# A two-layer graph network on one core: both layers in one program body, the first E tiles made ready earlier, and softmax row sums from fp16 halves

## The reference

```python
h = relu(layernorm(x))
x = x + A @ (h @ W0 + b0) / deg[:, None]          # A = (adj != 0), deg = column sums of A
h = relu(layernorm(x))
ht = (h @ W1) per head                            # 4 heads of 512
e = leaky_relu(src[:, None] + dst[None, :], 0.01) + adj
att = softmax(e, axis=-1)
x = x + mean over heads of att @ ht
```

## Time and profile before

| what | value |
|---|---|
| median of 3 runs | 2573.07 us |
| the profiled execution, its own time | 2572.89 us |
| its span, first to last instruction | 2571.2 us |
| TensorE busy | 2484.8 us, 97% |
| VectorE busy | 1878.0 us, 73% |
| ScalarE busy | 1244.6 us, 48% |
| GpSimd busy | 82.5 us, 3% |
| granted TensorE clock, mean | 0.979 |

### The profile page before, as it was taken

One profiled execution on the slowest core, in us unless ns is written; L12 is line 12 of the kernel. 1 busy time (PEld: TensorE's weight loads), 2 busy tenths in 40 slices (PEclk: granted clock), 3 DMA queues, 4 the chain that ended last, 5 costly groups with the idle time before them and its releaser, 6 DMA issues.

```text
span 2571.2 us, 42822 instructions
## 1 busy us (share of the span) xinstructions
PE 2484.8 (97%) x12301; PEld 1234.5 (48%) x12301; DVE 1878.0 (73%) x2621; ACT 1244.6 (48%) x1850; POOL 82.5 (3%) x132
## 2 busy tenths in 40 slices
PE   6989999599999999999999999999999999999997
PEld 3434446444444444444444444444444444444786
DVE  7779756497677876778677776777766877667774
ACT  4534544464444544445445454454444554444563
POOL 0000000000000000000000000000000000000000
PEclk9999998599999999999999999999999999999999
DMA  4175655400022000220002100021000300001000
GB/s 143 52 247 183 226 157 181 152 4 4 0 66 64 27 4 0 81 71 4 4 8 82 62 4 4 17 84 51 4 4 24 94 33 2 2 17 43 26 1 9
DMA packets 74145, 144.18 MB, mean 56 GB/s; under 512 B 4414, under 2 KB 11840, under 8 KB 72895
## 3 DMA queue, kind: packets, MB, share of 16 engines
q1 hardware_dynamic: 74047, 143.08, 17.4%
HBM read 129.37 MB, written 13.70 MB: 56 GB/s over the span
## 4 chain that ended last, share of the span: by engine, by line
PE 79%; issue 0%; DVE 0%; ACT 0%; POOLq 0%; POOL 0%
PE z_ps L1266 68%; PE o_ps L1290 11%; PE c_ps L1281 1%; DVE t_reg L1172 0%; ACT e_reg L1059 0%; DVE e_reg L1160 0%; DVE hl_reg L1138 0%; DVE ao_reg L1212 0%; DVE z_reg L1188 0%; ACT z_reg L1095 0%; POOLq L1029 0%; POOL ticks L1030 0%; POOLq L1030 0%; POOLq L352 0%
## 5 line engine op out<-in xcount | busy, mean ns | idle before, releaser
L1266 PE MATMUL z_ps<-hl_reg,h_reg 128*128 (+2 forms) x8736 | 1758.4, 364 | 23.9 <-DVE hl_reg L1138 23.9
L1266 PEld LDWEIGHTS z_ps<-hl_reg,h_reg 128*128 (+1 forms) x8736 | 855.3, 98 | 923.5 <-DVE hl_reg L1138 24.2
L1083 ACT ACTIVATE hl_reg<-t_reg (+2 forms) x364 | 361.7, 994 | 744.2 <-DVE t_reg L1172 399.8
L1138 DVE TENSOR_TENSOR hl_reg<-t_reg,hl_reg (+2 forms) x364 | 417.5, 1147 | 229.3 <-ACT hl_reg L1083 227.2
L1068 ACT ACTIVATE t_reg<-ring_reg,vv 128x512 f32 (+3 forms) x728 | 526.4, 770 | 71.0 <-DVE ao_reg L1153 59.0
L1172 DVE SCALAR_TENSOR_TENSOR t_reg<-t_reg,vv,e_reg (+3 forms) x728 | 510.4, 742 | 14.0 <-issue 8.2
L1153 DVE TENSOR_TENSOR ao_reg<-ao_reg,t_reg 128x1024 f32<-128x1024 f32 (+1 forms) x336 | 383.7, 1142 | 0.0
L1290 PE MATMUL o_ps<-w_reg,z_reg 128*128 128x512 f16 x1248 | 273.9, 379 | 0.6 <-DVE z_reg L1188 0.6
L1290 PEld LDWEIGHTS o_ps<-w_reg,z_reg 128*128 128x128 f16 x1248 | 121.9, 99 | 141.7 <-DVE z_reg L1188 0.7
L1188 DVE SCALAR_TENSOR_TENSOR z_reg<-z_ps,z_reg 128x512 f16<-128x512 f32 (+1 forms) x112 | 73.2, 653 | 147.6 <-ACT z_reg L1095 147.6
L1059 ACT ACTIVATE e_reg<-e_reg (+2 forms) x91 | 90.7, 996 | 176.1 <-DVE e_reg L1160 176.1
(11 more groups left out here) (126 smaller groups left out, 1072.0 us busy)
## 6 DMA issues: line engine op xcount, KB each, us to landing
ring_reg<-adjT_in SPq DMA_DIRECT2D x78, 512.0 KB, 4.2
e_reg<-adjT_in SPq DMA_DIRECT2D x78, 512.0 KB, 3.7
ring_reg<-x_in SPq DMA_DIRECT2D x13, 512.0 KB, 4.1
x_dram<-ring_reg SPq DMA_DIRECT2D x13, 512.0 KB, 6.4
ring_reg<-c_dram SPq DMA_DIRECT2D x24, 256.0 KB, 3.2
ao_reg<-x_dram SPq DMA_DIRECT2D x6, 1024.0 KB, 5.6
out_dram<-ao_reg SPq DMA_DIRECT2D x6, 1024.0 KB
w_reg<-W_in SPq DMA_DIRECT2D x5, 1024.0 KB, 9.7
```

Of the source, the lines that this page charges most:

```text
L1083: nc.scalar.activation(hl_ring[:, g % HL_RING, 0, :, 0:W], t_ring[:, g % T_RING, :, 0:W], ACT.Copy).then_inc(hi_ready, 1)
L1138: nc.vector.tensor_tensor(hl_ring[:, g % HL_RING, 1, :, 0:W], t_ring[:, g % T_RING, :, 0:W], hl_ring[:, g % HL_RING, 0, :, 0:W], ALU.subtr ...
L1266: mm = nc.tensor.matmul(z_ps[:, k, 0:W], hk[hs], hl_ring[:, r, ps, u, 0:W], start=first and u == 0 and n == 0, stop=last and u == 1 and n ...
```

## The change

1. The second block is gone. Its five engine programs become functions (`layer2_sync`, `layer2_gpsimd`, `layer2_scalar`, `layer2_vector`, `layer2_tensor`) that are called at the end of each engine's program in the first block, so that no engine waits there for all others. The memsets that give the semaphores their first credits stand at the start of VectorE's program. SyncE waits for the last stores of x1 before it reads `c` back, not after.
2. GpSimd's ticks are semaphore increments instead of adds. One add, `warm`, stands behind the last `partition_all_reduce`.
3. For block 0, VectorE subtracts the maximum from the E tiles of pairs 0 to 3 before the scores are taken out of PSUM, and of pairs 4 to 6 behind the tail's last VectorE instruction. It waits for the DMAs itself there. ScalarE takes the exponentials of pairs 0 to 3 before those of the tail (L804), and 4 to 6 after the copy (L808). Inside the first segment the rest follow two pairs ahead.
4. The row sums: `p_acc` is scaled by 2^-5 and split into fp16 halves at the end of a segment, by one ScalarE and one VectorE instruction (128x512) placed behind those that take out the last bank. TensorE does 8 fp16 matmuls in place of 4 fp32 ones, and does them behind the first 12 matmuls of the product instead of ahead of them.

```diff
-COEF = 1.0 / (ZS * HS * WS * H)
+RS = 2.0 ** -5
+COEF = RS / (ZS * HS * WS * H)
...
+acc16 = p_acc[:, :, 1].bitcast(F16).rearrange("p a (s i) -> p a s i", s=2)
...
+        E_PRE = LOOP0 + 2
+        E_PRE0 = 4
...
             if h == 0 and isinstance(b, int) and b == 0:
-                return (b, p + 1) if looped or p < PAIRS - 1 else None
+                return (b, p + E_PRE - LOOP0) if looped else None
...
             def pairs_here(b, p0, p1):
                 for p in range(p0, p1):
                     pool.wait_ge(e_in[p], (b + 1) * 16)
                     pool.wait_ge(mb_in, (b + 1) * 16)
-                    nc.gpsimd.tensor_tensor(ticks[:, p:p + 1], ones32[:], ones32[:], ALU.add).then_inc(e_here, 1)
+                    pool.sem_inc(e_here, 1)
...
         def subtract_max(dve, b, p):
+            if isinstance(b, int) and b == 0 and isinstance(p, int):
+                dve.wait_ge(e_in[p], 16)
+                dve.wait_ge(mb_in, 16)
+            else:
                 dve.wait_ge(e_here, b * PAIRS + p + 1)
...
             def evacuate(b, h):                     # ScalarE
...
+                act.wait_ge(acc_sum, q + 1)
+                nc.scalar.activation(acc16[:, h % 2, 0, 0:W], p_acc[:, h % 2, 0, 0:W], ACT.Copy,
+                                     scale=RS).then_inc(acc_hi, 1)
...
             def evacuate_z(b, h):                   # VectorE
...
+                dve.wait_ge(acc_hi, q + 1)
+                nc.vector.scalar_tensor_tensor(out=acc16[:, h % 2, 1, 0:W], in0=p_acc[:, h % 2, 0, 0:W],
+                                               scalar=RS, in1=acc16[:, h % 2, 0, 0:W], op0=ALU.mult,
+                                               op1=ALU.subtract).then_inc(acc_lo, 1)
...
-                pe.wait_ge(acc_sum, q + 1)
-                pe.wait_ge(rs_sb, q + 1)
-                for it in range(n):
-                    mm = nc.tensor.matmul(c_ps[:, it:it + 1], p_acc[:, h % 2, 0, it * P:(it + 1) * P],
-                                          ones32[:], start=True, stop=True)
-                mm.then_inc(rs_ps, 1)
+            def row_sums(b, h):
+                pe.wait_ge(acc_lo, q + 1)
+                pe.wait_ge(rs_sb, q + 1)
+                for it in range(width(b) // P):
+                    for s in range(2):
+                        mm = nc.tensor.matmul(c_ps[:, it:it + 1], acc16[:, h % 2, s, it * P:(it + 1) * P],
+                                              ones16[:], start=s == 0, stop=s == 1)
+                mm.then_inc(rs_ps, 1)
...
                     mm.then_inc(o_done, 1)
+                    if it == 0:
+                        row_sums(b, h)
...
                 nc.gpsimd.partition_all_reduce(dall[:], dmx[:], P, RMAX).then_inc(s_dall, 1)
+                nc.gpsimd.tensor_tensor(warm[:], ones32[:], ones32[:], ALU.add)
+                layer2_gpsimd(pool)
...
                 for j in pairs_of(NG1 - 1):
                     split1(j)
+                for p in range(E_PRE0):
+                    subtract_max(dve, 0, p)
                 dve.wait_ge(sd_ps, NT)
...
                 max_rows(1, IT)
+                for p in range(E_PRE0):
+                    exp_e(act, 0, p)
                 act.wait_ge(s_dn, 1)
```

More of the change, by code:

```diff
@@ L133, in gnn_kernel @@
         credits = sb("credits", 16, F32)
-        ticks = sb("ticks", PAIRS, F32)
+        warm = sb("warm", 1, F32)
         bst = sb("bst", NT * 6, F32)
@@ new lines, in o_before, with e_of @@
+        def o_before(b, h):
+            if isinstance(b, int) and b == FULL:
+                return FULL * H * IT + h * (LASTW // P)
+            return (b * H + h) * IT
+        def e_of(b, h, p):
+            looped = not isinstance(p, int)
+            if h == 0 and isinstance(b, int) and b == 0:
+                return (b, p + E_PRE - LOOP0) if looped else None
+            if h == 0:
+                return (b, p + E_LATE) if looped or p == LOOP0 - 1 else None
+            if h == H - 1 and (not isinstance(b, int) or b < FULL):
+                return (b + 1, p - LOOP0) if looped else None
+            return None
@@ new lines, in blocks, with exp_e, subtract_max @@
+        def blocks(eng, body, first=0):
+            for b in range(first):
+                body(b)
+            with eng.Fori(first, FULL - 1) as b:
+                body(b)
+            body(FULL - 1)
+            body(FULL)
+        def exp_e(act, b, p):
+            W = width(b)
+            act.wait_ge(e_sub, b * NT + p * 2 + 2)
+            e = e_blk[:, bass.ds(p * 2, 2), 0:W]
+            nc.scalar.activation(e, e, ACT.Exp).then_inc(e_ready, 1)
+        def subtract_max(dve, b, p):
+            W = width(b)
+            if isinstance(b, int) and b == 0 and isinstance(p, int):
+                dve.wait_ge(e_in[p], 16)
+                dve.wait_ge(mb_in, 16)
+            else:
+                dve.wait_ge(e_here, b * PAIRS + p + 1)
+            for u in range(2):
+                e = e_blk[:, p * 2 + u, 0:W]
+                nc.vector.tensor_tensor(e, e, max_bc[:, 0:W], ALU.subtract).then_inc(e_sub, 1)
@@ new lines, in layer2_gpsimd, with pairs_here, add_halves, body @@
+        def layer2_gpsimd(pool):
+            def pairs_here(b, p0, p1):
+                for p in range(p0, p1):
+                    pool.wait_ge(e_in[p], (b + 1) * 16)
+                    pool.wait_ge(mb_in, (b + 1) * 16)
+                    pool.sem_inc(e_here, 1)
+            def add_halves(b, h):
+                W = width(b)
+                pool.wait_ge(acc_done, (b * H + h + 1) * PAIRS + T_RING)
+                nc.gpsimd.tensor_tensor(p_acc[:, h % 2, 0, 0:W], p_acc[:, h % 2, 0, 0:W], p_acc[:, h % 2, 1, 0:W],
+                                        ALU.add).then_inc(acc_sum, 1)
+            pairs_here(0, 0, PAIRS)
+            def body(b):
+                for h in range(H - 1):
+                    add_halves(b, h)
+                more = not isinstance(b, int) or b < FULL
+                if more:
+                    pairs_here(b + 1, 0, LOOP1 - LOOP0)
+                add_halves(b, H - 1)
+                if more:
+                    pairs_here(b + 1, LOOP1 - LOOP0, PAIRS)
+            blocks(pool, body)
@@ L436, in _ @@
                 sp.dma_start(c_dram.rearrange("h (t i) -> (h t) i", i=P), c_st[0:H * NT]).then_inc(cr_out, 16)
+                for i in range(PAIRS - ADJ_RING, PAIRS):
+                    sp.wait_ge(x1_out[(NA + i) % ADJ_RING], 16 * (i // ADJ_RING + 1))
                 sp.wait_ge(cr_out, 16)
@@ L439, in _ @@
                     load_c(sp, 0, h)
[L440 to L441 removed]
                 sp.wait_ge(mr_out, 48)
                 load_x1(sp, 0)
+                layer2_sync(sp)
             @block.gpsimd
@@ L687, in _ @@
                 link(dve, nc.vector.tensor_scalar(vv4[:, 2], vv4[:, 0], -1.0, None, ALU.mult))
+                for p in range(E_PRE0, E_PRE):
+                    subtract_max(dve, 0, p)
+                layer2_vector(dve)
             @block.scalar
@@ L808, in _ @@
                 nc.scalar.activation(c_st[0:H * NT], o_ps[0:H * NT, 0, 0:P], ACT.Copy).then_inc(cr_sb, 1)
+                for p in range(E_PRE0, E_PRE):
+                    exp_e(act, 0, p)
+                layer2_scalar(act)
             @block.tensor
```

595 lines of the change are left out of this document (272 added, 323 removed).

## The result

The changed kernel takes **2547.09 us** (median of 4 runs, 2546.13 to 2548.46) against 2572.86 for the kernel before on the same chip (4 runs): ratio 0.9901, 95% interval 0.9884 to 0.9918. That is 25.8 us less.

What follows compares the result with a forecast made beforehand. TensorE, busy 97% of the span, was taken to bound the kernel, so only its wait before the segments and the row sums could pay: 2572.9 - 10.0 - 9.1 = 2553.8 us, range 2548 to 2562.

Steps and rivals of the forecast that it cites:

- The bound: Whole kernel: TensorE, busy 97% of the span, sets the time; its one long wait, 23.9 us, precedes the segments.
- The seam: From the tail to the segments' first matmul: TensorE starts at 501.1 in place of 511.14, 10.0 us less.
- My bound for neither `vv` nor `c` moving: Tail to segments: with both unmoved, TensorE would start at 497.6, 13.5 us less.
- The row sums: In each segment: 8 fp16 passes take 0.42 us in place of 0.79; 9.1 us less over all.
- 53 ns a pass: fp16 row sums: the clock-scaled part of a 98 ns weight load sets each pass's pace; the other 45 ns overlap.
- The rival: Row sums nearly free, a pass at half of 53 ns or less: 0.2 us a segment, 2549 us, chance 0.12.
- Layer 0: Work before the segments: the forecast sum has no term for a change in its length.
- What I costed at nothing: Segments: one more ScalarE and VectorE instruction each, 0.6 and 0.69 us, hidden under 5.7 us of cover, 2.9 in narrow ones.
- The range: Whole time: 2548 to 2562 us, from nearly free row sums up close to row sums that give nothing.
- The bound itself (a pass that costs nothing, -20): Row sums: if a pass cost nothing, they would give 20 us less.

Runs made afterwards that it cites:

- e2: The kernel before with one edit, GpSimd's ticks as semaphore increments instead of adds: 2564.05 us (6 runs), 0.9965 of before.
- e3: The changed kernel with the two blocks back, so that all engines meet between the tail and the segments: 2547.49 us.
- e10: The changed kernel with ScalarE's exponentials of E for pairs 0 to 3 moved behind the copy, pairs 4 to 6 into the first segment: 2544.93 us (4 runs).
- e15: The kernel of e10 run again, side by side with e14: 2544.16 us (4 runs).
- e6: The changed kernel with 24 more fp16 one-column passes in each segment, weights of 128 columns, results never read: 2564.91 us.
- e7: The changed kernel with 24 more fp16 one-column passes in each segment, weights of 127 columns: 2588.24 us.
- e12: The changed kernel with 24 more fp16 one-column passes in each segment, weights of 96 columns: 2577.32 us.
- e9: The changed kernel with 24 more fp16 passes of 128 moving columns in each segment: 2584.78 us.
- e8: The changed kernel with 24 more fp32 one-column passes (12 matmuls) in each segment, weights of 128 columns: 2661.46 us.
- e14: The changed kernel itself run again, side by side with e15: 2547.84 us (4 runs).
- e4: The changed kernel without GpSimd's add `warm`: 2547.15 us.

## Why the prediction was wrong, step by step

- **The bound**, TensorE alone in the segments and one long wait at the seam: right. The 10.38 and 67.34 us of a period are the same before and after.
- **The seam**, 10.0 us forecast, 10.27 measured. The chain is the forecast one: `vv` from 485.62 to 488.15 with the last split 1.24 us earlier, so 3.8 us later (forecast 3.9); `rows_c` 3.3 us later (forecast 3.5); `c` 3.2 us after it is asked for; 5.2 us from `c` to TensorE (forecast 5.2). e2 shows that the ticks alone carry 9.6 of it, e3 that the meeting carries 0.15, e10 that the exponentials ahead of `c` cost 3.0 of what else would be gained. My bound for neither `vv` nor `c` moving, 13.5 us less, is nearly what e10 reaches (13.3) and e15 (12.9).
- **The row sums**, "53 ns a pass": the step that failed. Forecast 9.1 us less, measured 15.25 over all segments. With 0.18 us a segment the sum gives 24 x 0.61 + 3 x 0.26 - 0.1 = 15.3. The term was mis-sized: the row sums take 0.18 us a segment, 22.5 ns a pass, where I had 0.42. I had taken the part of a load's recorded length that changes with the clock, 53 of 98 ns, for the pace of a stream of loads, and only the other 45 for what overlaps. e6, e7 and e12 show what sets the price: a pass with the full 128 fp16 columns costs 24 ns, and with fewer the price goes column by column, about one cycle of 2.4 GHz each, 43 ns for 96 and 57 for 127. The 53 ns are near the price of the slower load, for one that takes the faster. Whether that faster load sets the 24 ns or something else that no pass here went below was not separated. The recorded length is 72 to 85 ns above the price in every kind of one-column pass that was run; I had let 45 ns of it overlap.
- **The rival.** I had the right number beside me. The Trainium skill (TensorE: Matmul & The Clock Gate, Back-to-back issue gap) gives about 25 ns for a matmul of 1 to 64 columns, and its section Weight-path perf modes says that a fast load is used for 128 weights of a type other than fp32. Both agree with the traces: 24 ns, and 57 with 127 columns. The first section's 81 ns for a stream with 128 moving columns does not agree with e9, 56 ns. I gave the rival of nearly free row sums a chance of 0.12 because the 53 seemed to come from this case's rows, and it is what came. I had also summed it wrongly. At 0.2 us a segment, 24 x 0.59 + 3 x 0.24 - 0.2 is 14.7 us less, so that the whole is 2548.2, and not the 2549.6 that stands beside the 25 ns, nor quite the 2549 of the rival, which leaves the narrow segments out.
- **Layer 0**, costed at nothing, was 1.24 us shorter in the profiled execution. Nothing shows that as an effect of the change: the last split of the tail started between 475.26 (e8) and 479.48 us (e7) in kernels whose first layer is the changed kernel's, and at 477.27 in e14, the changed kernel again; the kernel before (478.08) and e2 (478.14) lie inside that spread. It did not put the time outside the range either. The forecast with the measured row sums alone is 2572.9 - 10.0 - 15.3 = 2547.6, with the measured seam too 2547.3, and the median is 2547.09.
- **What I costed at nothing** cost nothing: TensorE waits for no half in any segment but the last, where I had +0.2 us and 0.1 was measured.
- **The range** reached to 2548 because I put the nearly free row sums at 2549 with the seam as forecast. Summed rightly that rival lay at 2548.2, on the edge, with no room for the seam or for the spread between executions. The bound itself (a pass that costs nothing, -20) lay much lower, at 2543.

## What to carry to other kernels

When matmuls with one moving column stream, what each costs depends on its weights: on the type, on the number of columns, and on whether an fp16 load fills all 128. The length that the profile records for the load was 72 to 85 ns more than that price here. Splitting an fp32 operand into two fp16 halves costs work on other engines and still pays here, where those engines have slack and TensorE does not. And before a meeting of engines is blamed for a gap, ask which single instruction ends last: here a 128x1 add, put in only to increment a semaphore, held TensorE for 9.6 us (e2).

## What the runs showed of the hardware that I had not expected

- GpSimd's first add behind a `partition_all_reduce` has a start-up of 7.0 us in the changed kernel and 9.0 in the one before, with no instruction recorded for it. Semaphore increments behind it go out without one (e2), and with 72 us of waiting ahead of the add it doesn't show (e4).
- The granted clock fell to 0.50 behind 2.8 us of one-column passes, nearly all fp32, although TensorE is recorded as busy all the time (e8).
- How long the granted clock stays at 0.50 behind TensorE's start differs between executions, under 3 us in e14 and over 5 in e15, which is 1.3 us of time.
- fp32 passes cost 107 ns with 128 columns and 62 with 64. Why half the columns don't halve the price stays open.
